# Queries from high and low parts, and work moved off VectorE, in a fused linear-attention and channel-mixing kernel

## What is computed

```
a = layernorm(x)
q = a @ Wq + bq;  k = (a @ Wk + bk) @ Wc @ We;  v likewise        # 16 query heads, 4 key heads of 16
qf, kf = elu(q) + 1, elu(k) + 1
num = qf . cumsum(kf outer v);  den = qf . cumsum(kf) + 1e-6      # causal linear attention
y = a + (num / den) @ Wo + bo
x2 = x + layernorm(y) * gamma + beta
z = layernorm(x2)
xr, xk = mu * z + (1 - mu) * (z one token earlier)
out = x2 + sigmoid(xr @ W_r.T) * (relu(xk @ W_k.T) ** 2 @ W_v.T)
```

## Time and profile before

| | us |
|---|---|
| three timed runs | 290.34, 289.49, 290.89 (median 290.34) |
| the profiled execution, whole | 289.32 |
| its span, first to last instruction | 287.6 |
| PE busy | 263.5 (92%) |
| DVE busy | 239.6 (83%) |
| ACT busy | 151.9 (53%) |
| POOL busy | 130.6 (45%) |

### The profile page before, as it was taken

The page is one execution under the profiler, slowest core; times in us unless marked ns, Lnnn a source line. Parts: engine busy times, 40 slices in busy tenths (PEclk is TensorE's granted clock), DMA queues, the critical chain, the costliest instruction groups (busy, mean ns, idle before and its releaser), DMA issues.

```text
span 287.6 us, 7543 instructions
## 1 busy us (share of the span) xinstructions
PE 263.5 (92%) x2961; PEld 188.9 (66%) x2961; DVE 239.6 (83%) x588; ACT 151.9 (53%) x305; POOL 130.6 (45%) x152
## 2 busy tenths in 40 slices
PE   6987988966999999999999999999999899977794
PEld 6745557634885598558875788558855776744663
DVE  6587597899699989998999899996999778988523
ACT  2385675371555864386628845685148610444540
POOL 2628522124953567445644584356435322273210
PEclk9999999995699999999999999999999999999999
DMA  6810120000200022000400020002000110002112
GB/s 167 269 45 28 49 75 2 2 1 3 73 2 2 0 81 69 1 3 24 125 2 2 3 73 2 0 3 76 1 2 2 45 32 0 1 2 73 36 36 73
DMA packets 12178, 10.73 MB, mean 37 GB/s; under 512 B 2288, under 2 KB 12144, under 8 KB 12144
## 3 DMA queue, kind: packets, MB, share of 16 engines
q1 hardware_dynamic: 11392, 9.97, 10.7%
q10 hardware_dynamic: 752, 0.30, 0.4%
HBM read 6.07 MB, written 4.19 MB: 36 GB/s over the span
## 4 chain that ended last, share of the span: by engine, by line
PE 76%; DVE 13%; issue 4%; POOL 3%; ACT 2%; DMA 1%; DVEq 0%; POOLq 0%; ACTq 0%
PE ps_x L459 10%; PE ps_x L381 8%; PE ps_z L430 6%; PE ps_x L474 6%; PE ps_x L481 6%; PE ps_y L446 5%; PE ps_y L451 5%; PE ps_x L375 5%; PE ps_z L481 4%; PE ps_x L499 4%; PE ps_x L467 3%; PE ps_z L474 3%; PE ps_x L368 2%; DVE probs L984 2%; PE ps_z L413 2%
## 5 line engine op out<-in xcount | busy, mean ns | idle before, releaser
L984 DVE TENSOR_TENSOR probs<-ps_z,causal 128x512 f32<-128x512 f32 x64 | 40.8, 679 | 4.7 <-PE ps_z L430 4.7
L459 PE MATMUL ps_x<-wo_sb,oT 128*128 128x256 f32 x128 | 29.6, 382 | 0.0
L277 POOL TENSOR_TENSOR out_tok<-tanh_r,x_tok 128x512 f32<-128x512 f32 x14 | 18.7, 1340 | 23.7 <-DVE tanh_r L1057 23.4
L254 POOL TENSOR_TENSOR xb_tok<-x_in,beta_bc 128x1024 f32<-128x1024 f32 x8 | 18.9, 2362 | 20.7 <-DVE x_tok L1030 20.7
L381 PE MATMUL ps_x<-aT,wq_sb 128*128 128x512 f32 x60 | 27.8, 605 | 0.0
L262 POOL TENSOR_TENSOR prod<-qf,ksum 128x1024 f32<-128x1024 f32 x6 | 14.1, 2355 | 29.5 <-DVE ksum L954 29.5
L459 PEld LDWEIGHTS ps_x<-wo_sb,oT 128*128 128x128 f32 x128 | 23.7, 191 | 3.8 <-issue 0.9
L217 POOL TENSOR_TENSOR rstd<-rstd,neg_half 128x4 f32<-128x4 f32 x24 | 25.1, 1045 | 1.9
L430 PE MATMUL ps_z<-qf,kfT 32*128 32x128 f32 x512 | 23.8, 300 | 1.4 <-ACT rden_bc L709 0.5
L446 PE MATMUL ps_y<-qf,state 32*32 32x128 f32 x512 | 20.9, 278 | 2.9 <-DVE oT L998 2.4
L446 PEld LDWEIGHTS ps_y<-qf,state 32*32 32x32 f32 x512 | 12.1, 105 | 17.1 <-issue 11.8
(11 more groups left out here) (143 smaller groups left out, 606.9 us busy)
## 6 DMA issues: line engine op xcount, KB each, us to landing
x_in<-in_L_attn_x_dram SPq DMA_DIRECT2D x8, 512.0 KB, 4.3
out_dram<-out_tok SPq DMA_DIRECT2D x16, 256.0 KB, 2.1
xr<-in_L_attn_Wq_dram ACTq DMA_DIRECT2D x1, 256.0 KB, 4.2
xk<-in_L_ffn_W_r_dram SPq DMA_DIRECT2D x1, 256.0 KB, 5.5
xk<-in_L_ffn_W_k_dram SPq DMA_DIRECT2D x1, 256.0 KB, 5.7
xr<-in_L_ffn_W_v_dram SPq DMA_DIRECT2D x1, 256.0 KB, 6.3
wo_sb<-in_L_attn_Wo_dram SPq DMA_DIRECT2D x4, 64.0 KB, 4.9
bo_bc<-in_L_attn_bo_dram SPq DMA_DIRECT2D x1, 128.0 KB, 5.5
```

The costliest lines, as they stand in the source:

```text
L254: PL.tensor_tensor(xb_tok[n % 2][:], x_in[n % XBUF][:], beta_bc[:].unsqueeze(1).to_broadcast([P, NB, D]), ALU.add).then_inc(s_xb, 1)
L459: last = mm(bk_[:, (b % 2) * D:(b % 2 + 1) * D], oT[m % 2][:, a, b, :], wo_sb[:, a, :], start=(a == 0), stop=(a == 1))
L984: V.tensor_tensor(probs[b % 2][:, 2 * h:2 * h + 2, :].rearrange("p g (r s) -> p g r s", s=HALF), ps_z[:, 2 * h:2 * h + 2, 0:2 * P].rearran ...
```

## The change

The queries of chunks 1 to 7 come from three fp32r products (high by high, high by low, low by high), as W_v's already do. `wq_sb` is split once, on ACT and DVE; `aT` is split in every step: two copies of 128x512 on ACT behind `a_out`, two differences of 128x512 on DVE (`low_a`) behind `key_features`. DVE writes `kf` once, and ACT doubles it (`double_keys`), from chunk 1 on. Each mask is one instruction over four banks. On POOL, in the full steps, `add_bo` goes ahead of `first_norm`; in step 1 the `prod` of the denominators goes from POOL to DVE, and `centre` goes behind the last mask; in the finale `second_norm(c)` goes ahead of `finish(f)` on POOL, and `normalise_z(c)` ahead of `gate_r(m, 0)` on ACT.

```
+            def query_parts(n, a, bk_):
+                pe.wait_ge(s_aTh, 2 * n)
+                for k in range(KD):
+                    for part in range(2):
+                        mm(bk_[:, :], wq_p[part][:, k, a, :], aT_p[0][:, k, :], start=(k == 0 and part == 0), stop=False)
+                pe.wait_ge(s_aTl, 2 * n)
+                for k in range(KD):
+                    last = mm(bk_[:, :], wq_p[0][:, k, a, :], aT_p[1][:, k, :], start=False, stop=(k == KD - 1))
+                last.then_inc(s_q_ps, 1)
...
             def keys_transposed(n):
                 pe.wait_ge(s_kf, 2 * n + 2)
+                if n >= 1:
+                    pe.wait_ge(s_kd, n)
...
+            def double_keys(n):
+                act.wait_ge(s_kf, 2 * n + 2)
+                copy(kf[:, :, :, 1, :], kf[:, :, :, 0, :]).then_inc(s_kd, 1)
...
+                for k in range(KD):
+                    act.wait_ge(s_aT, 2 * n + k + 1)
+                    copy(aT_p[0][:, k, :], aT[:, k, :]).then_inc(s_aTh, 1)
...
+            def low_a(n):
+                for k in range(KD):
+                    dve.wait_ge(s_aTh, 2 * n - 1 + k)
+                    V.tensor_tensor(aT_p[1][:, k, :], aT[:, k, :], aT_p[0][:, k, :].bitcast(F32), ALU.subtract).then_inc(s_aTl, 1)
...
             def mask(c, b):
-                for h in range(2):
-                    dve.wait_ge(s_sc, 8 * c + 2 * b + h + 1)
+                dve.wait_ge(s_sc, 8 * c + 2 * b + 2)
...
                 key_features(n)
+                low_a(n)
                 divide(c, 0)
                 mask(c, 2)
                 queries(n, 0, x0)
-                if m >= 0:
-                    centre(m)
                 queries(n, 1, x1)
                 divide(c, 1)
                 states(n)
                 key_sums(n)
-                if m < 0:
-                    denominator_terms(n)
+                denominator_terms(n)
                 mask(c, 3)
                 if m >= 0:
+                    centre(m)
                     second_residual(m)
```

More of the change, by code:

```diff
@@ L102, in build @@
                       for name, shape in (("ka", (2, T)), ("wv", (KD, D))))
+        s_kd = sem("kf_doubled")
+        aT_p, wq_p = ([ctx.enter_context(nc.sbuf_tensor(f"{name}_{part}", [P, *shape], F32R)) for part in ("high", "low")]
+                      for name, shape in (("aT", (KD, T)), ("wq", (KD, 2, P))))
+        s_aTh, s_aTl, wq_split = sem("aT_high"), sem("aT_low"), sem("wq_split")
         s_kah, s_kal, wv_split = sem("kact_high"), sem("kact_low"), sem("wv_split")
@@ L285, in step @@
                     norm_x(n + 1)
-                if m >= 0:
-                    first_norm(m)
                 if f >= 0:
                     add_bo(n)
+                    first_norm(m)
                     add_beta(n)
@@ L313, in finale @@
                 token_difference(m)
+                second_norm(c)
                 finish(f)
-                second_norm(c)
                 finish(m)
@@ L544, in step @@
                 pe.wait_ge(s_kv, 2 * n + 2)
-                queries(n, 0, x0)
+                pe.wait_ge(wq_split, 2)
+                query_parts(n, 0, x0)
                 if f >= 0:
@@ L551, in step @@
                     pe.wait_ge(ffn_w_sb, 1)
-                queries(n, 1, x1)
+                query_parts(n, 1, x1)
                 outputs(c, 1)
@@ L822, in step @@
                     gate_r(f, 0, x1)
+                double_keys(n)
+                if f >= 0:
                     gate_r(f, 1, x2)
@@ L857, in finale @@
                 channel_k(m, 1, z1)
+                normalise_z(c)
                 gate_r(m, 0, z2)
-                normalise_z(c)
                 gate_r(m, 1, z3)
@@ L897, in _ @@
             act.wait_ge(pool_const, 3)
+            copy(flat(wq_p[0]), flat(wq_sb)).then_inc(wq_split, 1)
             for c in range(LAST):
@@ L937, in key_features @@
                 dve.wait_ge(s_ekm, n + 1)
-                for j in range(2):
+                for j in range(1 if n else 2):
                     V.scalar_tensor_tensor(out=kf[:, :, :, j, :], in0=kb[:].rearrange("p b (g d) -> p b g d", d=HD),
                                            scalar=1.0, in1=ek[:].rearrange("p b (g d) -> p b g d", d=HD),
-                                           op0=ALU.add, op1=ALU.max).then_inc(s_kf, 1)
+                                           op0=ALU.add, op1=ALU.max).then_inc(s_kf, 2 if n else 1)
             def queries(n, a, bk_):
@@ L981, in mask @@
                     dve.wait_ge(s_o, 4 * c + b - 1)
-                for h in range(2):
-                    dve.wait_ge(s_sc, 8 * c + 2 * b + h + 1)
-                    V.tensor_tensor(probs[b % 2][:, 2 * h:2 * h + 2, :].rearrange("p g (r s) -> p g r s", s=HALF),
-                                    ps_z[:, 2 * h:2 * h + 2, 0:2 * P].rearrange("p g (r s) -> p g r s", s=HALF),
-                                    causal[:].unsqueeze(1).unsqueeze(1).to_broadcast([P, 2, 4, HALF]),
-                                    ALU.mult).then_inc(s_pr, 1)
+                dve.wait_ge(s_sc, 8 * c + 2 * b + 2)
+                V.tensor_tensor(probs[b % 2][:].rearrange("p g (r s) -> p g r s", s=HALF),
+                                ps_z[:, :, 0:2 * P].rearrange("p g (r s) -> p g r s", s=HALF),
+                                causal[:].unsqueeze(1).unsqueeze(1).to_broadcast([P, G, 4, HALF]),
+                                ALU.mult).then_inc(s_pr, 2)
             def divide(c, b):
@@ L1066, in step @@
                     norm_x(n + 1)
+                if c == 0:
+                    dve.wait_ge(wq_split, 1)
+                    V.tensor_tensor(wq_p[1][:], wq_sb[:], wq_p[0][:].bitcast(F32), ALU.subtract).then_inc(wq_split, 1)
                 if f < 0:
```

## The result

The changed kernel took a median of 292.76 us in four timed runs (292.06 to 293.49). The kernel before, timed beside it, took 290.05 (289.49 to 290.89). The ratio is 1.0096, 95% interval [1.0064, 1.0129]: slower by about 1%, and just outside the range that was forecast. The profiled execution took 292.06 us, with a span of 290.2, so it is compared with a span of 287.6 before.

The account below looks back on a forecast made before the run. PE was taken to bound the full steps, DVE close behind, but not step 1 or parts of the finale. Terms -3.0 + 2.4 + 0.9 - 1.1 - 0.1 = -0.9 gave 289.4 us against the 290.34 median; range 286.4 to 292.2.

Parts of the forecast that it names:

- Full steps: Five steps, c = 2 to 6: PE relieved, `mix_k` starts about 0.6 us earlier; -0.6 each, -3.0 in all.
- The late-stall case: Full steps: if the stall of `centre` beside `abo_tok` stayed, DVE 0.7 us late and the gain 0.
- Price: +2.4: Step 0: `abo_tok` gets between the two `low_a` differences, PE waits for the low parts; +2.4 us.
- The collision itself: Step 0: POOL's `abo_tok` holds up DVE's second difference some 2.2 us, so it ends at about 35.2.
- rival B: Step 0: the collision also drops PE's clock to 1.2 GHz, +2.5 us more, 291.9 us in all; chance 18%.
- Nothing, at most 0.3: Ahead of step 0's keys: splitting `wq` on ACT and DVE is hidden while both wait for PE; 0 to 0.3 us.
- Step 1: DVE-bound stage: later `qf`, idle time and added `prod`, less a collision of `second_residual`; +0.9 us, bounds 0 and +1.5.
- Finale: `out_tok` no longer collides with `xk` and `second_residual`; -1.1 us, bounds -0.3 and -1.9, masks a further -0.1.
- the masks, for which I had put 0.1: Finale: masks as single instructions were to gain 0.1 us.

Follow-up runs that it names:

- `abo_tok` late: Changed kernel with POOL's `add_bo` behind `first_norm` again in the full steps: 300.58 us, ratio 1.0377.
- the first two experiments: Changed kernel with step 0's `abo_tok` waiting for both differences, 288.72 us; changed kernel with 13 extra products filling PE's wait in step 0, 291.12 us.
- the one with the exchanged `xk`: Changed kernel with DVE's second `qf` between the two `xk` of a full step instead of behind both: 291.45 us, ratio 1.0027.
- the kernel with both repairs of step 0: Changed kernel with step 0's `abo_tok` waiting for the differences and `wq_low` moved from DVE to POOL: 287.99 us, ratio 0.9948.
- Relief alone: Changed kernel with the queries as fp32 products again, no parts, copies or differences; all else stays: 290.38 us, ratio 0.9999.
- the old order: Changed kernel with POOL's and ACT's order in the finale as before the change: 292.36 us, ratio 1.0085.
- the first experiment: Changed kernel, but in step 0 POOL's `abo_tok` waits for the two differences of `low_a` instead of `kf`: 288.72 us, ratio 0.9965.
- halves of a change: Changed kernel with fp32 queries again, no parts: 290.38 us; kernel before with the queries from parts and none of the moves: 300.89 us.

## Why the prediction was wrong, by its own steps

**Full steps: right in mechanism and nearly in size.** Forecast -0.6 each, measured -0.51. `centre` at 1.66, the products 0.23 apart, and `mix_k` waiting on the chain over the second `qf` and no longer on PE came as predicted, except that PE is idle for 0.08 us there (its scores end at 160.44, `mix_k` starts at 160.52) and not for 0.2. The queries took 2.9 us, not 2.8, and the full step 30.26, not 30.15. The first of the five, step 2, gained 0.7. The late-stall case I had taken as a bound of 0 was measured at +0.8 (`abo_tok` late), so that bound was too mild, though it wasn't needed.

**Step 0: the step of the sum that failed.** I wrote "Price: +2.4" for it, and it measured +5.0: the term held the wait alone. The collision itself was foretold well: PE was to wait from 32.0 to 35.2 and waited from 32.7 to 36.0, with one difference at 2.83 us. On its own it costs 2.15 us (the first two experiments), against my 2.3. Two things were missing. The first is the clock, 2.2 us. I had it as rival B, at 18%, and argued against it that step 1 needed more idle time, and that "the gap in step 0 has full work on both sides". The first of these is a misreading of the earlier trace rows. PE had stood idle for 2.91 us up to 65.30 and then worked to 65.94, and the kernel before still had its clock in this window (PE's busy time, then the granted clock):

```profile
65.00:66.00 1.00, 0.64 (x16) 0.99 0.00 0
```

From 66 us on it was at 0.50. So step 1 had lost its clock behind a shorter wait than the 3.2 us that I expected in step 0, and the row spoke for rival B. The second had no measurement behind it: in the changed kernel PE was busy without a gap from 26.67 to 32.70 us, and the clock fell 2.0 us into the wait all the same.

All seven kernels here that have the collision, and don't fill the wait, had a fall between 34.6 and 37.2 us; the other seven have none there. Step 0 lasted 26.9 to 27.3 us in each of the seven. They are not all alike, though. In the changed kernel and the one with the exchanged `xk` the clock fell within the wait, for 6.8 us. In the other five it fell only behind the wait, for 3.4 us, and four of these had another 3.4 us at 26.5 to 26.8, ahead of the collision (in the kernel with both repairs of step 0, such an early fall alone cost 0.94: 23.45 against 22.51). So the 2.2 us are the clock's price in the changed kernel's trace, and not in every execution. The case that I held at 18% was the one to forecast. Its sum, -0.9 + 2.5 = +1.6 us, has 4.9 us in step 0, where 5.0 were measured. That it comes so near is partly luck: it has 2.4 + 2.5 for wait and clock, where 2.15 + 2.2 were measured, and 0.65 of the stage that it lacks make up for this. The rest of the distance to the +2.6 in the spans is spread over the prologue (0.5), step 1 (0.3) and the full steps (0.3).

The second is the split of `wq_sb`. "Nothing, at most 0.3" rested on both engines having to wait for PE at that place. They did, but POOL did not: its norm runs there, and `wq_low` collided with it. That is 0.44 us by the runs, and the last 0.2 of the 0.65 (22.95 - 22.30) I did not take apart. The rule that I had applied correctly one paragraph later (an instruction of DVE with two operands in SBUF against POOL) was not applied to the added instruction that I thought hidden, nor to the small POOL instructions, which can be the ones that wait.

**Step 1: right.** +0.9 forecast, +1.2 measured, of which 0.82 is the order (shown by putting it back) and 0.35 left open.

**Finale: right.** Forecast -1.2 with the masks, measured -1.3; `xk`, `x_tok` at their undisturbed times. Relief alone gives the same 59.57, so nothing of it is due to the parts; and with the old order 1.3 is lost again, so nothing measurable is due to the masks, for which I had put 0.1.

**Prologue.** It took 0.5 us more after. In the thirteen other traces it lies between 20.69 and 22.12, and kernels with the same prologue differ in it (20.72 in the first experiment, 21.16 in the changed kernel, without a fall of the clock in either), so I put nothing on it. Why it varies stays open.

**The sum again, from what was measured:** -2.76 (five full steps) + 5.03 + 1.17 - 1.32 + 0.47 = +2.59 us of span; 4.4 of the 5.03 hang on one wait of POOL. The forecast had the sign of each stage, and was off by the size of a single one. The gain that the change holds is real: with that wait, `wq_low`, the order in step 1, and that of `xk` and `qf` put right, the same idea takes 285.43 us.

## What to carry to other kernels

Where an instruction with two operands in SBUF is added on DVE, list every POOL instruction that can be waiting or running beside it, the four-element ones too, and the other way round; it is the semaphore that POOL waits on, not the amount of work, that decides who gets in between. Cut a change into stages before judging it: here one wait hid the gains of the full steps and the finale, and halves of a change that each gain nothing (+0.03 and +1.05 a step) gained 0.51 together. And where a new wait on TensorE is some 3 us long, price it twice, once as time and once as half-speed work behind it: here the clock fell in or behind it in seven kernels of seven, and in the changed kernel this was as large as the wait (2.2 beside 2.15).

## What the runs showed of the hardware that I had not expected

**The granted clock falls at other places in other executions of the same program.** The kernel before, 23 executions on one chip, mostly fell into groups: 288.95 and 289.03 us at a mean clock of 0.991, ten between 289.37 and 289.67 at 0.982, four of 290.67 to 290.96 at 0.976, and three of 292.33 to 292.41 at 0.971. The other four don't fit this order (289.67 and 289.74 at 0.975, 290.22 and 290.32 at 0.985), so the mean clock alone doesn't give the time, and why isn't shown. Between executions of one unchanged kernel lie 3.5 us, and a comparison of two single runs can be off by as much. In the profiled executions the fall in step 1 was there in all but the two kernels that fill PE's waits in that stage; others came in the prologue, in step 0, or in the finale (in the first experiment, behind a wait of 2.17 us for `xk`, so that its finale took 61.27 us instead of 59.56; the changed kernel has the same wait of 2.17 us, and no fall behind it). In the kernel with both repairs of step 0 it fell at 27 us. The windows of PE in that kernel, us and busy time, then the granted clock:

```profile
24.00:25.00 1.00, 0.48 (x16) 1.00 0.00 0
25.00:26.00 1.00, 0.83 (x15) 1.00 0.00 0
...
27.00:28.00 1.00, 1.00 (x12) 0.50 0.07 10
```

No wait in front of it was longer than 1.09 us, and work lay between them. A patchy stretch did what I had thought only one long wait does. It did so in five of the fourteen profiled executions; the changed kernel has the same waits at this place, 1.09 and 0.55 us, and kept its clock there.

**The small POOL instructions are held up too.** A difference of 0.68 us took 2.83 with a POOL instruction of 2.35 us between; POOL's own instruction was recorded at 2.72 instead of 2.37; and a four-element one at 0.65 instead of 0.21 behind a DVE instruction. The Trainium skill (SBUF — State Buffer, "Who interferes with whom") has the rule that the first to issue blocks the other, and the trace agrees. The turn-taking of large ones was in the forecast; that a scale of four elements in the chain of a norm pays for it was not.

**A mask over four PSUM banks gains less than the count suggests.** One instruction of 128x1024 takes 1.209 us, and the pair of 128x512 took 1.25 to 1.29: 0.05 to 0.08 for a saved instruction.
